# Writing out VectorE's one-hot loop and spreading a layer-1 post step over four pairs in a graph kernel

## What is computed

```python
dinv = rsqrt(degree of each node)
for l in range(3):                              # three graph convolutions
    hw  = h @ W[l].T
    agg = segment_sum(hw[src] * dinv[src] * dinv[dst], dst)
    h   = h + elu(agg + b[l])
x1 = layernorm(x + concat(h0..h3) @ lin_w.T + lin_b)
# then a relational layer: gather x1[src] * weight, sum by (relation, dst), two small products
out = layernorm(x1 + relational(x1))
```

## Time and profile before

| | us |
|---|---|
| median of 3 runs | 1109.1 |
| lowest and highest | 1108.51, 1109.41 |
| the profiled execution, its own time | 1110.03 |
| its span, first to last instruction | 1108.2 |

### The profile page before, as it was taken

How to read it: one execution, slowest core, us unless ns; L and a number is a source line. 1 busy time by engine, 2 the same in 40 slices (tenths; PEclk the granted TensorE clock), 3 DMA queues, 4 the chain that set the end, 5 groups by cost and what they waited for, 6 DMA issues and landing times.

```text
span 1108.2 us, 23482 instructions
## 1 busy us (share of the span) xinstructions
PE 1013.3 (91%) x9508; PEld 665.9 (60%) x9508; DVE 802.2 (72%) x1702; ACT 444.9 (40%) x1027; POOL 510.5 (46%) x542
## 2 busy tenths in 40 slices
PE   1677898889999999999399999999999999999997
PEld 1565565556644475448266666666666666666664
DVE  4689999898526764898786677777677777767753
ACT  1588898888400030004443233233233333333320
POOL 5044000000047700000377777777777777777773
PEclk9877999899999999999589999999999999999999
DMA  5263000000101010010522222222222222222221
GB/s 155 57 193 87 7 1 2 1 1 1 59 15 27 18 59 1 1 58 14 134 54 54 59 54 58 60 54 58 59 54 58 59 53 58 59 51 58 58 53 36
DMA packets 48801, 55.34 MB, mean 50 GB/s; under 512 B 15543, under 2 KB 39129, under 8 KB 48182
## 3 DMA queue, kind: packets, MB, share of 16 engines
q0 software_dynamic: 16240, 31.95, 11.5%
q1 hardware_dynamic: 32454, 21.87, 6.9%
HBM read 42.10 MB, written 8.49 MB: 46 GB/s over the span
## 4 chain that ended last, share of the span: by engine, by line
PE 68%; DVE 18%; issue 6%; SPq 2%; ACT 2%; DMA 2%; DVEq 1%; POOL 0%
PE ps L1684 21%; PE ps L1537 21%; PE ps L1663 11%; PE ps L1678 9%; DVE arena L1107 8%; SPq L681 2%; PE ps L1526 2%; DVE dinv_all L1336 2%; DVE hT L1296 1%; PE ps L1697 1%; PE ps L1691 1%; DVE u L1330 1%; PE ps L1484 1%; DMA dinv_col<-dinv_scratch 1%; DVE arena L1259 1%
## 5 line engine op out<-in xcount | busy, mean ns | idle before, releaser
L837 POOL DMA_INDIRECT arena<-x_scratch,arena x437 | 413.4, 946 | 164.6 <-issue 126.2
L1537 PE MATMUL ps<-arena,u 125*128 125x480 fp8e5 (+1 forms) x1575 | 361.3, 356 | 1.2 <-ACT arena L891 1.2
L972 ACT COPY arena<-ps 125x400 f32<-125x400 f32 x364 | 170.2, 525 | 354.6 <-PE ps L1678 325.6
L1684 PE MATMUL ps<-arena,u 125*128 125x448 f32 x650 | 297.8, 539 | 0.0
L1537 PEld LDWEIGHTS ps<-arena,u 125*128 125x128 bf16 x1575 | 153.1, 98 | 108.1 <-ACT arena L891 1.7
L1663 PE MATMUL ps<-hT,arena 128*128 128x160 f32 x874 | 200.0, 321 | 2.6 <-DVE hT L1296 2.1
L1107 DVE TENSOR_TENSOR arena<-arena 128x2048 bf16<-128x2048 bf16 (+2 forms) x158 | 188.7, 1253 | 16.5 <-PE ps L1526 13.4
L1663 PEld LDWEIGHTS ps<-hT,arena 128*128 128x128 f32 x874 | 144.1, 190 | 87.3 <-issue 74.1
L1526 PE MATMUL ps<-arena 128*128 128x125 bf16 x1256 | 150.5, 234 | 32.4 <-DVE arena L1107 30.7
L1678 PEld LDWEIGHTS ps<-dinv_all,u 64*128 64x128 bf16 x4368 | 109.1, 96 | 103.5 <-issue 82.8
L1526 PEld LDWEIGHTS ps<-arena 128*128 128x128 bf16 x1256 | 108.2, 105 | 86.0 <-DVE arena L1107 47.9
(11 more groups left out here) (187 smaller groups left out, 712.9 us busy)
## 6 DMA issues: line engine op xcount, KB each, us to landing
arena<-x_scratch,arena POOLq DMA_INDIRECT x437
arena<-hT SPq DMA_DIRECT2D x2, 1562.5 KB, 7.1
edge_scratch<-arena SPq DMA_DIRECT2D x5, 403.0 KB, 5.2
arena<-in_x_dram SPq DMA_DIRECT2D x1, 1562.5 KB
dinv_all<-dinv_scratch SPq DMA_DIRECT2D x1, 1562.5 KB, 8.3
h_scratch<-hT SPq DMA_DIRECT2D x1, 1562.5 KB, 6.1
first_term_scratch<-arena SPq DMA_DIRECT2D x1, 1562.5 KB
arena<-first_term_scratch SPq DMA_DIRECT2D x1, 1562.5 KB
```

The costliest lines, as they stand in the source:

```text
L837: nc.gpsimd.indirect_dma_start(out=gat[:, j, :], out_offset=None, in_=x1_d, in_offset=bass.IndirectOffsetOnAxis(ap=idxg[:, j:j + 1], axis= ...
L972: nc.scalar.copy(o, ps[0:BLK, octet_bank(k, w), 0:4 * ND].rearrange("p (i m) -> p m i", i=4)).then_inc(s_se, 1)
L1537: return T.matmul(ps[:, agg_bank(l, c), 0:CW[c]], u[0:BLK, s, k, :], region[:, s, 0:CW[c]], start=(first and s == 0 and k == 0), stop=(end ...
L1684: last = T.matmul(ps[:, 5, 0:NB * DN].rearrange("p (b n) -> p b n", b=NB), xb[0:BLK, s, :], sD[half][0:BLK].rearrange("p (b v) n -> p b v ...
```

## The change

The hardware loop over pairs is replaced by written-out code, so that waits and addresses are constants. `post` gets a list of steps, and in chunks 2 to 6 step 0 (L1146) comes behind the one-hots of pair 2, step 1 (L1148) behind pair 3, step 2 (L1150, L1151) behind pair 4 and step 3 (L1153) behind pair 5. The two `wpos` operations of chunk 4 come behind pair 7. ScalarE's `exps` comes behind the writes of pair 2. The waits of chunk 2 on earlier loads stay behind pair 1.

```diff
-                if c >= 2:
-                    exps(0, c - 2)
                 for i in range(1, (GPC if c < NCH - 1 else LASTG) // 2):
                     for slot in range(2):
                         write_block(c, i, slot)
+                    if c >= 2 and i == 2:
+                        exps(0, c - 2)
...
+                if 0 in steps:
+                    dve.wait_ge(s_agg, NCH * l + c + 1)
+                    V.tensor_tensor(z, ps[:, agg_bank(l, c), 0:w], dinv_all[:, at:at + w], ALU.mult).then_inc(s_rd, 1)
+                    dve.wait_ge(s_rd, 2 * NCH * l + 2 * c + 1)
+                if 1 in steps:
+                    V.tensor_scalar(m, z, b, 0.0, ALU.add, ALU.min).then_inc(s_rd, 1)
+                    dve.wait_ge(s_rd, 2 * NCH * l + 2 * c + 2)
+                if 2 in steps:
+                    link(V.tensor_scalar(z, z, b, 0.0, ALU.add, ALU.max))
+                    link(V.tensor_tensor(h, h, z, ALU.add))
+                if 3 in steps:
+                    dve.wait_ge(s_exp, NCH * l + c + 1)
+                    V.scalar_tensor_tensor(h, m, -1.0, h, ALU.add, ALU.add).then_inc(s_h, 1)
+                    dve.wait_ge(s_h, NCH * l + c + 1)
...
             for c in range(1, NCH):
-                for pair in range(2):
-                    onehots(GPC * c + 2 * pair, pair, False)
-                if c == 2:
-                    dve.wait_ge(s_u, NUB)
-                    dve.wait_ge(s_hs, 16)
-                    dve.wait_ge(s_dinva, 16)
-                if c >= 2:
-                    post(0, c - 2)
-                if c == 4:
-                    dve.wait_ge(s_stl, 224)
-                    link(V.tensor_scalar(wposf[:, :, :], wposf[:, :, :], 0.0, float(E - NW), ALU.max, ALU.min))
-                    V.tensor_copy(wpos[:, :, :], wposf[:, :, :]).then_inc(s_wpos, 1)
-                with dve.Fori(1, (GPC if c < NCH - 1 else LASTG) // SLOTS) as i:
-                    for pair in range(2):
-                        onehots(i * SLOTS + (GPC * c + 2 * pair), pair, False)
+                for t in range((GPC if c < NCH - 1 else LASTG) // 2):
+                    onehots(GPC * c + 2 * t, t % 2, False)
+                    if c == 2 and t == 1:
+                        dve.wait_ge(s_u, NUB)
+                        dve.wait_ge(s_hs, 16)
+                        dve.wait_ge(s_dinva, 16)
+                    if c >= 2 and 2 <= t < 6:
+                        post(0, c - 2, (t - 2,))
+                    if c == 4 and t == 7:
+                        dve.wait_ge(s_stl, 224)
+                        link(V.tensor_scalar(wposf[:, :, :], wposf[:, :, :], 0.0, float(E - NW), ALU.max, ALU.min))
+                        V.tensor_copy(wpos[:, :, :], wposf[:, :, :]).then_inc(s_wpos, 1)
```

More of the change, by code:

```diff
@@ L1137, in parts, with post @@
                 dve.wait_ge(s_u, NUB * l + NUB)
-            def post(l, c):
+            def post(l, c, steps=range(4)):
                 w, at = CW[c], CH * c
```

## The result

| | before | changed |
|---|---|---|
| median, us | 1109.26 (4 runs) | 1094.89 (4 runs) |
| lowest and highest | 1108.51, 1111.59 | 1094.02, 1097.32 |
| profiled execution | 1110.03 | 1097.32 |
| its span | 1108.2 | 1095.4 |

The ratio is 0.9874, with a 95% interval of 0.9852 to 0.9896. The forecast was 1096.8, in a range of 1094 to 1102.

The account below looks back on a forecast made before the run. No engine was full in the build, VectorE nearest, with VectorE and TensorE waiting in turn. Gains of 11.4 (chunks 2 to 5), 0.5 and 0.5 made 12.4 us: 1097.6 off the profile, 1096.7 off the median; stated 1096.8, range 1094 to 1102.

Parts of the forecast that it names:

- The ring: Build: VectorE's one-hots and TensorE's builds wait in turn over two buffers; two pairs fall from 4.71 to 4.58 us.
- The spread steps: Chunks 2 to 5: post pieces between pairs keep VectorE full; pairs 2 to 6 take 12.08 us, a chunk 30.40.
- The waits put at nothing: Build: the moved steps and ScalarE's exponential find their inputs ready or covered, so their waits cost nothing.
- The fourth rival: A wait put at nothing, or longer VectorE code, loses 2 to 6 us: 1099 to 1103; chance 0.12.
- the third: Rival: writing out leaves the wait on TensorE at 4.71 us for two pairs, only spreading gains: 1099.3; chance 0.14.
- The clock: TensorE's granted clock stays 1.00 from 104 to 285 us, with idle gaps of at most 1.2 us.
- the first rival: Build: the clock still falls once in each chunk, giving 4.4 to 6.8 us back: about 1102; chance 0.10.
- the second: Rival: the clock falls between the spread pairs and stays low, slower than before, about 1119 us; chance 0.04.
- the clock's play: Behind the build: low-clock stretches may fall otherwise on the shifted stages, bounded by one us each way.
- the build's start and chunk 6: No gain counted at the build's start; chunk 6's 0.48 us hole behind the post step goes, 0.5 us.
- Chunk 1's five iterations: Chunk 1: five loop iterations at 0.13 us each are saved, put at 0.5 us (0 to 1.0).
- the prediction's 0.2% for what a measurement tells: A measurement of this kernel was taken to tell 0.2% (2.2 us) from no change.

Follow-up runs that it names:

- e2: The changed kernel with the spread steps kept, but pairs 6 to 11 (2 to 11 of chunk 1) in the hardware loop again: 1099.37 us, ratio 0.9915.
- e1: The changed kernel with the whole post step and ScalarE's exponential put back as a block, only the one-hots written out: 1099.67 us, ratio 0.9919.
- e8: The kernel before, loop and block kept, with 11 unread matmuls on TensorE ahead of pair 2's build in chunks 2 to 5: 1301.63 us, ratio 0.9942, another chip.
- e3: e1 with 11 unread matmuls more on TensorE ahead of pair 2's build in chunks 2 to 5: 1097.13 us, ratio 0.9897.
- before once more: The kernel before, unchanged, run once for a second profile on the same chip as e8: 1310.11 us.
- the second set: The changed kernel once more (1096.16 us) and three variants of it, run on one chip beside before at 1107.9 us.
- e5: The changed kernel with a post step of four VectorE operations in place of five: 1094.84 us, ratio 0.9871.
- e6: The changed kernel with unread matmuls of zeros on TensorE ahead of the relational layer and behind its first eight octets: 1093.07 us, ratio 0.9864.

## Why the prediction was right

Point by point.

**The ring.** Forecast 4.58 us for two pairs written out. From 171.04 to 175.60, which is the next pair but one, it is 4.56; the loop's 4.70 is gone. The reading that the wait through registers was a part of the ring, and the loop's branch was not, holds by e2's rows: 4.69 and 4.71 us with the register step, 4.56 without, and the branch under a comparison. No run has one of the two without the other.

**The spread steps.** Forecast 12.08 us from pair 2 to pair 6; measured 171.04 - 158.98 = 12.06 in chunk 3. The other eight pairs: forecast 18.32, measured 18.20, since the last two, around the chunk's border, take 4.51 and not the ring's 4.56. A chunk is 30.27 for 30.40, and the four together 121.30 for 122.0. The two `wpos` operations cost 0.2, not 0.4.

**The waits put at nothing.** ScalarE's exponential stood ready: no VectorE line in the timeline above waits for it. The fourth rival falls on that, and the third on the ring's 4.56, where it had 4.71.

**The clock.** Forecast 1.00 from 104 to 285 us, TensorE's longest idle time behind step 2 of 1.2 us; measured 1.00 from 104 us to the build's end, and 1.09 in chunk 3 (1.10 at most). The Trainium skill's case of micro-idles that make the clock oscillate (TensorE: Matmul & The Clock Gate, A second HAM failure mode) did not show here: four gaps of 0.32 to 1.09 us in a row left it at the high level. So the first rival falls, and with it the second, slower than before, which had the same ground. The prediction's plain link of stall and fall was too strong, though: e1's stall of 2.64 us was followed by a low stretch in one chunk and by none in another.

**What was off.** First, I had no term for what the clock costs in before as such; it was inside the difference of the chunks. Cut from pair 2 to pair 2, the four stretches of chunks 2 to 5 sum to 132.4 us before, 125.4 with the clock held up (e8), 122.0 written out too (e3) and 121.3 spread. So of the 12.1 us the clock is 7.0, writing out 3.4 and the spreading at full clock 0.7; the last 1.1 is the wait for the exponential behind the table load of chunk 2, for which VectorE stood inside the block and no longer does. Each of these is one profile: by before once more, on e8's chip, the four sum to 134.6, and the clock's part would be 9.2. The spreading's work is to keep the clock, and written-out one-hots do a part of that as well: alone each gave 7 to 8 us by the medians (e1, e2), together 12 to 14. Second, the stages behind the build: I had bounded the clock's play at one us each way, and it took 0.9 in the profile. Third, the build's start and chunk 6 gave 0.39 and 0.65 where I had 0 and 0.5. Chunk 1's five iterations of 0.13 are 0.65, which I had put down as 0.5; its eleven pairs gave 0.54. Sum: 13.7 in the build for 12.4. That the profiled execution came out at 1097.32, beside the 1097.6 worked out for it, is in part luck: 1.3 us more in the build and 0.9 us less behind it nearly cancel.

The median moved by 14.4 us, more than the profiled executions (12.7). The four runs of the changed kernel lie 3.3 us apart and the profiled one is the slowest. What its faster runs did otherwise was not profiled. In the second set the medians lie 11.7 us apart, and before's own runs there 9.8. So the distance of a median from the forecast says little below some 2 us, and the prediction's 0.2% for what a measurement tells was too tight.

## What to carry to other kernels

A block of work on one engine that starves TensorE is cheap if that engine is the full one, and stays so; here it cost 0.2 us, and the clock that fell behind it 1.5 and more. So compare TensorE's busy time for the same instructions between stretches first, and ask of a stall what it does to the clock before asking how to hide it. Cutting the block into pieces and giving TensorE idle work in the gap brought nearly the same, and the pieces are free. Where two engines pass two buffers to and fro, add up the ring, waits through registers included: a tenth of a microsecond in it comes back for every turn. And look at every place that runs the code you shorten: e5's four operations won 1.7 us where they were spread and lost 1.0 where they stood as a block.

## What the runs showed of the hardware

- The rise of the clock doesn't move exactly with the kernel: the relational layer began 13.7 us earlier, the clock rose 11.5 us earlier, and 0.9 us was lost. The same code in one kernel (e1) had two chunks with a low stretch and two without, 1.5 us apart. The runs scatter with it: in the second set before's seven runs spread over 9.8 us, from 1103.73 at a mean granted clock of 0.967 to 1113.51 at 0.955. The changed kernel's four spread over 3.7, e6's over 2.9.
- The same kernel took 1108 to 1109 us in three sets of runs and 1309 us on another chip. The build was nearly the same there (32.5 to 34.2 us a chunk). The relational layer from the 34th tile to the last took 685 us in place of 528, with TensorE busy 559 of them; another 42 us of difference lie between the build and that tile. These are the two stretches, before and before once more:

```profile
569.50:1097.96 528.46, 526.13 (x5718) 348.71 (x5716) 366.31 (x1040) 165.94 (x370) 392.50 (x415) 1.00 0.22 56
```

```profile
612.82:1298.23 685.41, 559.20 (x5716) 374.10 (x5716) 370.04 (x1038) 165.21 (x372) 385.99 (x409) 0.93 0.16 43
```

Why that chip is slower there stays open; no experiment was made on it.
